# Softmax sums written to PSUM instead of SBUF, and their reciprocals taken in two steps

## The chip, the cores and the metric

The kernel runs on one core of a Trainium2 chip. A core has five engines that work side by side and wait for each other through semaphores: TensorE (PE in the profile; PEld is its loading of weights), VectorE (DVE), ScalarE (ACT), GpSimd (POOL) and SyncE (SP), which issues the transfers between the chip's memory and SBUF. TensorE writes its results to PSUM, eight banks of 2 KB in each of 128 partitions; VectorE and ScalarE read and write both PSUM and SBUF. The metric is the time of one execution on the device, in microseconds (us).

## The reference

The input `x` and the context are 128 batch rows of 128 tokens by 256 features. The attention has 16 heads of 16 features. Its softmax runs over axis 2, the queries (not the keys), so each key has a sum of its own:

```python
x = x + xattn(layernorm(x), ctx, Wq, bq, Wkv, bkv, Wo, bo)
    scores = einsum('bhqd,bhkd->bhqk', q, k) / sqrt(D)
    attn = softmax(scores, axis=2)               # over the queries
    out = einsum('bhqk,bhkd->bhqd', attn, v) @ Wo + bo
x = x + ffn(layernorm(x), w_router, w_block)
    top_idx = top_k(x @ w_router, 96 of 128 tokens)
    out = x with gelu(x[top_idx] @ w_block) put at top_idx
```

## The kernel before

A batch row is one step of a pipeline. Stage offsets are written into the loops by hand: in step s TensorE makes the scores of row s, transposes the inputs of row s + 5, makes the values of row s - 1, keys of row s + 2 or queries of row s + 3 (every other step), the output projection of row s - 2, the product with the block weights of row s - 4, and the attention of row s - 1. Each engine has its own instruction list in the order of the code, and carries it out in that order; nothing is scheduled at run time. A wait holds up everything behind it on its engine.

**Scores and softmax.** `scores(b)` (line 325) makes scores with the keys on the 128 partitions and the queries along the free axis. Its 16 heads lie in four blocks j = 0 to 3 of four heads, each block in one bank of `ps_s`: banks 1 to 3 for blocks 1 to 3 of every row; block 0 changes between bank 0 (even rows) and bank 4 (odd rows), as `bank(b, j)` says. VectorE takes each block's negated maximum over the queries (`maxima`, line 712), in the order 3, 2, 1, 0. ScalarE follows in the same order (`exps`, line 567): four exponentials a block, one for a head, 128 values on each partition, with the maximum as a bias. Each has an `accum_out`: the sum of its 128 results. On the chip that is a pair of instructions, the exponential (ACTIVATE) and the read of the accumulator (ACTIVATION_READ_ACCUMULATOR). The sums of a row lie in the SBUF tile `sums`, four rows deep. The fourth read of a block raises `exp_ready[j]`.

**The reciprocal.** Since the sum belongs to the key, the kernel divides the values and not the probabilities: VectorE takes the reciprocal of all 16 sums of row s - 1 in step s (`inverse_sums`, line 757), GpSimd multiplies the values with it (`values_over_sums`, line 1042), and the attention matmuls (line 402) use them.

**What holds the scores.** `scores(b)` may write its banks when row b - 1 has been read from them. As block 1 is the third to be done, a wait for `exp_ready[1]` covers blocks 3, 2 and 1; block 0 lies in the other bank.

**The router.** Every eighth step a group of eight rows goes through the choice of the 96 tokens. TensorE transposes the group's scores (`candidates`, line 481) into `ps_s`' fifth bank, VectorE finds the 32 smallest in four rounds of max and replace, spread over steps, and TensorE transposes the flags back (`keep_columns`, line 488). Both transposes wait for `exp_ready[0]`, since that bank also holds block 0 of odd rows.

A step of VectorE ends with `final` (line 868, the selected rows), `stats2` (line 735), `product_scaled` (line 815), and the next step begins with `x1_transposed` (line 721), statistics and the router's work, and then `maxima(s, 3)`.

Of the kernel before, what the change touches and what calls it, by code (L numbers as in the profile page):

```python
# [6 lines left out]
def cross_attention_routed_ffn(  # L7
# [40 lines left out]
    with ctx:  # L48
# [3 lines left out]
        def sem(name):  # L52
            return ctx.enter_context(nc.semaphore(name))
# [42 lines left out]
        sums = sb("sums", [P, 4, H])  # L96
# [25 lines left out]
        def bank(b, j):  # L122
            return J if j == 0 and b % 2 == 1 else j

# [49 lines left out]
        recip_ready = sem("recip_ready")  # L174
# [103 lines left out]
        def _(pe):  # L278
# [46 lines left out]
            def scores(b):  # L325

                if not has(b):
                    return
                r2, h = (b // 2) % 2, b % 2
                if b == 0:  # L330
                    pair_ready(b)
                if has(b - 1):
                    pe.wait_ge(exp_ready[1], upto(b - 1))
                for c in range(C):
                    for j in range(J):
                        rows = slice(32 * j, 32 * j + 32)
                        mm = nc.tensor.matmul(ps_s[:, bank(b, j), c, :, :], k_sb[rows, r2, c, h * T:(h + 1) * T],  # L337
                                              q_eo[rows, r2, :, c, h, :], start=True, stop=True)
                        if c == C - 1:
                            mm.then_inc(s_mm[j], 1)  # L340
# [134 lines left out]
            def candidates(b):  # L475

                if b % GROUP == 0 and has(b):
                    pe.wait_ge(z_ready, upto(b + 7))
                    pe.wait_ge(exp_ready[0], upto(b + 11))
                    r = b % R  # L480
                    nc.tensor.transpose(ps_cand, z_sb[:, r:r + GROUP, E], ident[:, :]).then_inc(score_mm, 8)

            def keep_columns(b):

                if b % GROUP == 0 and has(b):
                    pe.wait_ge(keep_row_ready, upto(b + 7))
                    pe.wait_ge(exp_ready[0], upto(b + 15))
# [63 lines left out]
        def _(act):  # L551
# [5 lines left out]
            def exps(b, j, settled=False):  # L557
# [6 lines left out]
                for c in range(C):  # L564
                    for par in range(2):
# [3 lines left out]
                                                    accum_out=sums[:, b % 4, h:h + 1])  # L569
# [108 lines left out]
        def _(dve):  # L678
# [73 lines left out]

            def inverse_sums(b):

                if has(b):
                    dve.wait_ge(exp_ready[0], upto(b))
                    nc.vector.reciprocal(recip[:, b % 4, :], sums[:, b % 4, :]).then_inc(recip_ready, 1)  # L757
# [141 lines left out]
            centre_block_weights()  # L899
            maxima(1, 3)  # L900
# [10 lines left out]
            queries(4)  # L911

            for s in range(2, B):
# [30 lines left out]
                final(s - 16, sure)  # L944
                stats2(s - 2)
# [264 lines left out]
```

## Time and profile before

| | us |
|---|---|
| median of 3 runs | 921.12 (920.46 to 921.23) |
| profiled execution, span from first to last instruction | 919.4 |
| TensorE busy | 889.4 (97%) |
| ScalarE busy | 879.5 (96%) |
| VectorE busy | 873.5 (95%) |
| GpSimd busy | 796.8 (87%) |
| exponentials, 2048, mean 411 ns | 719.1 |
| accumulator reads, 2048, mean 251 ns | 513.5 |
| reciprocals, 128, mean 238 ns | 30.4 |

The median and the range are times of runs without a profile; the span is that of one profiled execution, 1.7 us below the median. Instructions of one engine overlap in the profile: the next one starts before the last one's result is written. The exponentials and the reads add up to more than ScalarE's busy time for that reason. How long an instruction keeps its engine is read from the distance of two starts, and when its result is there from its own duration. In the rows of the section below "start us, us, engine line op out<-in xcount [idle before <-releaser]" are the columns of instructions in order of time; numbers of the form 128x512 are partitions by elements.

### The profile page before, as it was taken

The page shows a single profiled execution, that of the slowest core. Times are in us where ns is not written, and L with a number is a line of the kernel's source. Part 1 is how long each engine was busy: PE and PEld are TensorE (multiplying, and loading weights), DVE is VectorE, ACT ScalarE, POOL GpSimd, SP SyncE. Part 2 cuts the span into 40 slices and gives each one's busy share as a digit, 9 for nine tenths or more (in the row PEclk, how much of TensorE's full clock was granted, in tenths as well). Part 3 has the DMA queues.
Part 4 walks back from the last instruction along what each step waited for, and adds up shares of the span by engine and source line. Part 5 has one row for each costly group of instructions (what it writes and reads, how often), then busy time and mean ns, then how long its engine had stood idle before and what let it go on. Part 6 is the DMA issues. An engine that isn't in the chain of part 4 may idle for free. (4 is left out here: it accounts for less than half of the span.)

```text
span 919.4 us, 31003 instructions
## 1 busy us (share of the span) xinstructions
PE 889.4 (97%) x10306; PEld 753.9 (82%) x10306; DVE 873.5 (95%) x2320; ACT 879.5 (96%) x4503; POOL 796.8 (87%) x1488
## 2 busy tenths in 40 slices
PE   7899999999999999999999999999999999999973
PEld 6788888888888888888888888888888888888861
DVE  6899999999999999999999999999999999999887
ACT  5999999999999999999999999999999999999983
POOL 4568789999989999899999999999899999998865
PEclk9999999999999999999999999999999999999997
DMA  6222123223223223223223223223223222221102
GB/s 198 62 65 71 46 61 95 57 84 93 57 84 95 60 83 92 58 86 91 70 75 91 59 86 91 71 74 89 76 71 89 76 71 87 76 61 53 49 24 92
DMA packets 70976, 70.45 MB, mean 77 GB/s; under 512 B 12064, under 2 KB 62752, under 8 KB 70816
## 3 DMA queue, kind: packets, MB, share of 16 engines
q1 hardware_dynamic: 69456, 67.68, 25.5%
q8 instruction: 82, 1.34, 0.6%
q10 hardware_dynamic: 1360, 0.79, 0.3%
q14 instruction: 78, 0.64, 0.2%
HBM read 35.13 MB, written 16.78 MB: 56 GB/s over the span
## 5 line engine op out<-in xcount | busy, mean ns | idle before, releaser
L567 ACT ACTIVATE e_sb<-ps_s,neg_max 128x128 f32<-128x128 f32 x2048 | 719.1, 411 | 4.4 <-DVE neg_max L712 3.9
L567 ACT ACTIVATION_READ_ACCUMULATOR e_sb<-ps_s,neg_max 128x1 f32 x2048 | 513.5, 251 | 0.0
L712 DVE TENSOR_REDUCE neg_max<-ps_s 128x4 f32<-128x512 f32 x512 | 329.0, 663 | 26.4 <-PE ps_s L337 26.4
L337 PE MATMUL ps_s<-q_eo,k_sb 32*128 32x256 f32 x2048 | 146.6, 400 | 1.1 <-DVE k_sb L790 0.5
L402 PE MATMUL ps_a<-e_sb,v_pad 128*32 128x128 f32 x4096 | 138.4, 276 | 2.2 <-DVE x_sb L729 1.6
L299 PE MATMUL ps_a<-w_o_sb,o_sb 128*128 128x256 f32 x512 | 133.2, 382 | 2.0 <-DVE v_sb L803 1.9
L299 PE MATMUL ps_t<-w_z_sb,xt_sb 128*128 128x258 f32 x512 | 132.6, 381 | 1.3 <-DVE z_sb L815 1.3
L1042 POOL TENSOR_TENSOR v_pad<-v_sb,recip 128x256 f32<-128x256 f32 x128 | 79.6, 622 | 54.0 <-DVE recip L757 52.5
L402 PEld LDWEIGHTS ps_a<-e_sb,v_pad 128*32 128x32 f32 x4096 | 104.1, 109 | 24.0 <-issue 21.6
L337 PEld LDWEIGHTS ps_s<-q_eo,k_sb 32*128 32x128 f32 x2048 | 92.5, 184 | 29.4 <-ACT e_sb L567 17.0
L1031 POOL TENSOR_TENSOR x_sb<-x_sb,bo_sb 128x256 f32<-128x256 f32 x128 | 114.0, 892 | 0.2
L299 PEld LDWEIGHTS ps_t<-w_z_sb,xt_sb 128*128 128x128 f32 x512 | 97.3, 191 | 15.4 <-issue 1.8
L299 PEld LDWEIGHTS ps_a<-w_o_sb,o_sb 128*128 128x128 f32 x512 | 88.0, 189 | 10.1 <-issue 2.4
L1088 POOL TENSOR_TENSOR g_sb<-g_sb,z_sb 128x256 f32<-128x256 f32 x128 | 90.9, 710 | 0.3
L578 ACT CAST t_hi<-ps_t 128x512 fp32r<-128x512 f32 x126 | 74.2, 589 | 14.0 <-PE ps_t L366 10.5
L764 DVE TENSOR_TENSOR t_lo<-ps_t,t_hi 128x512 fp32r<-128x512 f32 x126 | 85.2, 676 | 1.4 <-ACT t_hi L578 1.4
L292 PE MATMUL ps_a<-w_v_hi,t_hi 128*128 128x256 f32 x256 | 84.4, 330 | 1.7 <-ACT o_sb L586 1.6
L1102 POOL TENSOR_TENSOR z_sb<-g_sb,z_sb 128x256 f32<-128x256 f32 x121 | 82.8, 685 | 0.0
L1071 POOL TENSOR_TENSOR g_sb<-z_sb 128x256 f32<-128x256 f32 x123 | 75.6, 614 | 0.3 <-DVE z_sb L815 0.3
L292 PE MATMUL ps_q<-t_hi,w_k_hi 128*128 128x256 f32 x252 | 71.2, 282 | 1.6 <-DVE q_raw L777 1.6
L292 PE MATMUL ps_a<-w_v_lo,t_hi 128*128 128x256 f32 x256 | 72.5, 283 | 0.0
L292 PE MATMUL ps_q<-t_hi,w_q_hi 128*128 128x256 f32 x256 | 72.3, 282 | 0.2 <-DVE t_lo L764 0.2
(102 smaller groups left out, 2197.6 us busy)
## 6 DMA issues: line engine op xcount, KB each, us to landing
x_sb<-in_x SPq DMA_DIRECT2D x64, 256.0 KB, 2.9
c_sb<-in_ctx SPq DMA_DIRECT2D x64, 256.0 KB, 3.1
out<-z_sb SPq DMA_DIRECT2D x64, 256.0 KB, 2.4
q_eo<-q_raw SPq DMA_DIRECT2D x504, 32.0 KB, 2.0
z_sb<-in_L_xattn_Wkv ACTq DMA_DIRECT2D x2, 256.0 KB, 7.2
z_sb<-in_L_xattn_Wq ACTq DMA_DIRECT2D x1, 256.0 KB, 4.5
w_z_sb<-in_L_ffn_w_block SPq DMA_DIRECT2D x1, 256.0 KB, 7.6
w_o_sb<-in_L_xattn_Wo SPq DMA_DIRECT2D x1, 256.0 KB, 7.0
```

Source lines behind the costliest of these rows:

```text
L292: last = nc.tensor.matmul(dst, lhs(a, c), rhs(b, c), start=(c == 0 and n == 0), stop=(c == C - 1 and n == len(terms) - 1))
L299: last = nc.tensor.matmul(dst, lhs(c), rhs(c), start=(c == 0), stop=(c == C - 1))
L337: mm = nc.tensor.matmul(ps_s[:, bank(b, j), c, :, :], k_sb[rows, r2, c, h * T:(h + 1) * T], q_eo[rows, r2, :, c, h, :], start=True, stop=True)
L402: mm = nc.tensor.matmul(ps_attn[32 * j:32 * j + 32, c * T:(c + 1) * T], v_pad[:, b % 2, c * J + j, par:par + 2, :].rearrange("p a d -> p ( ...
L567: last = nc.scalar.activation(e_sb[:, b % 4, j, c, par, :], ps_s[:, bank(b, j), c, par, :], ACT.Exp, bias=neg_max[:, b % 4, h:h + 1], accu ...
L712: nc.vector.tensor_reduce(neg_max[:, b % 4, :].rearrange("p (c j q) -> p j c q", c=C, j=J)[:, j, :, :], ps_s[:, bank(b, j), :, :, :], AX.X ...
L764: nc.vector.tensor_tensor(t_lo[part].rearrange("p k c t -> p (k c) t"), inputs_bank(b)[:, :].rearrange("p (n t) -> p n t", t=T), t_hi[part ...
L1031: nc.gpsimd.tensor_tensor(x_sb[:, b % R, :], x_sb[:, b % R, :], bo_sb[:, :], ALU.add).then_inc(xb_ready, 1)
L1042: nc.gpsimd.tensor_tensor(v_pad[:, b % 2, :, 0:3:2, :], v_sb[:, b % 2, :].rearrange("p (g q d) -> p g q d", q=2, d=D), recip[:, b % 4, :]. ...
L1071: nc.gpsimd.tensor_tensor(g_sb[:, b % 4, :], z_sb[:, b % R, 0:E], z_sb[:, b % R, 0:E], ALU.mult).then_inc(square_ready, 1)
L1088: nc.gpsimd.tensor_tensor(g_sb[:, b % 4, :], g_sb[:, b % 4, :], z_sb[:, b % R, 0:E], ALU.mult).then_inc(cubic_ready, 1)
L1102: nc.gpsimd.tensor_tensor(z_sb[:, b % R, 0:E], g_sb[:, b % 4, :], z_sb[:, b % R, 0:E], ALU.mult).then_inc(gelu_ready, 1)
```

## The change

Each exponential's sum is written into its own block of scores in PSUM, at the first column, which that exponential has just read. The tile `sums` goes. As the next row's scores overwrite banks 1 to 3, the reciprocals of blocks 1 to 3 are taken as 12 values after `final(s - 16)` in step s (`inverse_sums_123`), and the scores of the next row wait for them (`recip_123_ready`) in place of `exp_ready[1]`. Block 0's four are taken in the place of the old reciprocal, in the next step; the two router transposes wait for these (`recip_ready`) in place of `exp_ready[0]`.

```diff
+        def sums_of(b, js):
+            return ps_s[:, bank(b, js[0]):bank(b, js[0]) + len(js), :, :, 0]
...
             def scores(b):
                 if has(b - 1):
-                    pe.wait_ge(exp_ready[1], upto(b - 1))
+                    pe.wait_ge(recip_123_ready, upto(b - 1))
...
             def candidates(b):
-                    pe.wait_ge(exp_ready[0], upto(b + 11))
+                    pe.wait_ge(recip_ready, upto(b + 11))
             def keep_columns(b):
-                    pe.wait_ge(exp_ready[0], upto(b + 15))
+                    pe.wait_ge(recip_ready, upto(b + 15))
...
             def exps(b, j, settled=False):
-                                                    accum_out=sums[:, b % 4, h:h + 1])
+                                                    accum_out=ps_s[:, bank(b, j), c, par, 0:1])
...
+            def inverse_sums_123(b):
+                if has(b):
+                    dve.wait_ge(exp_ready[1], upto(b))
+                    nc.vector.reciprocal(recip[:, b % 4, :].rearrange("p (c j q) -> p j c q", c=C, j=J)[:, 1:J, :, :],
+                                         sums_of(b, (1, 2, 3))).then_inc(recip_123_ready, 1)
             def inverse_sums(b):
                 if has(b):
                     dve.wait_ge(exp_ready[0], upto(b))
-                    nc.vector.reciprocal(recip[:, b % 4, :], sums[:, b % 4, :]).then_inc(recip_ready, 1)
+                    nc.vector.reciprocal(recip[:, b % 4, :].rearrange("p (c j q) -> p j c q", c=C, j=J)[:, 0:1, :, :],
+                                         sums_of(b, (0,))).then_inc(recip_ready, 1)
...
             centre_block_weights()
+            inverse_sums_123(0)
             maxima(1, 3)
...
             queries(4)
+            inverse_sums_123(1)
             for s in range(2, B):
...
                 final(s - 16, sure)
+                inverse_sums_123(s)
                 stats2(s - 2)
```

VectorE's list around a step's end, in a step with router work, before (`z_sb<-z_sb` is the selection of final rows, `neg_max<-ps_s` the maxima, `recip` the reciprocal; the names behind "waits" are semaphores):

```order
L757 RECIPROCAL recip<-sums 128x16 [waits exp_ready0]
L712 TENSOR_REDUCE neg_max<-ps_s 128x2x2 [waits s_mm1]
L777 TENSOR_TENSOR q_raw<-ps_q,bq_sb 128x512 [waits q_mm]
L729 TENSOR_TENSOR x_sb<-ps_a,x_sb 128x256 [waits o_mm]
L712 TENSOR_REDUCE neg_max<-ps_s 128x2x2 [waits s_mm0]
L841 MAX top<-cand 8x8 [waits top_dropped]
L868 SCALAR_TENSOR_TENSOR z_sb<-z_sb,half_keep,x_sb 128x256 [waits u_ready]
L735 BN_STATS st<-x_sb 128x6 [waits x1_ready]
```

The same piece now:

```order
L767 RECIPROCAL recip<-ps_s 128x2x2 [waits exp_ready0]
L715 TENSOR_REDUCE neg_max<-ps_s 128x2x2 [waits s_mm1]
L788 TENSOR_TENSOR q_raw<-ps_q,bq_sb 128x512 [waits q_mm]
L732 TENSOR_TENSOR x_sb<-ps_a,x_sb 128x256 [waits o_mm]
L715 TENSOR_REDUCE neg_max<-ps_s 128x2x2 [waits s_mm0]
L852 MAX top<-cand 8x8 [waits top_dropped]
L879 SCALAR_TENSOR_TENSOR z_sb<-z_sb,half_keep,x_sb 128x256 [waits u_ready]
L760 RECIPROCAL recip<-ps_s 128x3x2x2 [waits exp_ready1]
L738 BN_STATS st<-x_sb 128x6 [waits x1_ready]
```

The reciprocal of 16 values has become one of four in its place, and one of twelve between the selection and the statistics, with a wait for ScalarE's block 1.

VectorE's list at the start, before, from the statistics ahead of row 2's key bias (`k_sb`) over the centring of the block weights (`w_z_sb`) to row 1's first maxima, and then from the query bias (`q_raw`) to row 2's first maxima:

```order
L790 TENSOR_TENSOR k_sb<-ps_q,bk_sb 128x512 [waits k_mm]
L704 TENSOR_TENSOR w_z_sb<-w_z_sb,ps_a 128x258 [waits w_mean_mm]
L704 TENSOR_TENSOR w_z_sb<-w_z_sb,ps_a 128x258
L712 TENSOR_REDUCE neg_max<-ps_s 128x2x2 [waits s_mm3]
...
L777 TENSOR_TENSOR q_raw<-ps_q,bq_sb 128x512 [waits q_mm]
L712 TENSOR_REDUCE neg_max<-ps_s 128x2x2 [waits s_mm3]
```

The same now:

```order
L801 TENSOR_TENSOR k_sb<-ps_q,bk_sb 128x512 [waits k_mm]
L707 TENSOR_TENSOR w_z_sb<-w_z_sb,ps_a 128x258 [waits w_mean_mm]
L707 TENSOR_TENSOR w_z_sb<-w_z_sb,ps_a 128x258
L760 RECIPROCAL recip<-ps_s 128x3x2x2 [waits exp_ready1]
L715 TENSOR_REDUCE neg_max<-ps_s 128x2x2 [waits s_mm3]
...
L788 TENSOR_TENSOR q_raw<-ps_q,bq_sb 128x512 [waits q_mm]
L760 RECIPROCAL recip<-ps_s 128x3x2x2 [waits exp_ready1]
L715 TENSOR_REDUCE neg_max<-ps_s 128x2x2 [waits s_mm3]
```

Twice a reciprocal has been put ahead of a row's first maxima, behind what VectorE does there.

TensorE's order is what it was; the semaphores in two places of it are others. Before (`ps_s<-q_eo` are the scores, `keep_row` the router's flags):

```order
L402 MATMUL ps_a<-e_sb,v_pad 32x128 x15
L337 MATMUL ps_s<-q_eo,k_sb 128x256 [waits exp_ready1]
...
L488 MATMUL ps_s<-ident,keep_row 128x8 [waits exp_ready0,keep_row_ready]
L299 MATMUL ps_a<-w_o_sb,o_sb 128x256 [waits v_ready]
L299 MATMUL ps_a<-w_o_sb,o_sb 128x256
```

And now:

```order
L405 MATMUL ps_a<-e_sb,v_pad 32x128 x15
L340 MATMUL ps_s<-q_eo,k_sb 128x256 [waits recip_123_ready]
...
L491 MATMUL ps_s<-ident,keep_row 128x8 [waits recip_ready,keep_row_ready]
L302 MATMUL ps_a<-w_o_sb,o_sb 128x256 [waits v_ready]
L302 MATMUL ps_a<-w_o_sb,o_sb 128x256
```

Both waits have moved from ScalarE's exponentials to VectorE's reciprocals.

## Rows read from the trace of the kernel before

**Rows 1.** Windows: busy us of each engine (instructions), TensorE clock, DMA, GB/s.

```profile
500.00:600.00 100.00, 100.00 (x1183) 84.75 (x1181) 97.77 (x260) 98.77 (x515) 92.74 (x173) 1.00 0.29 84
```

**Rows 2.** In order of time: TensorE's scores in two following steps.

```profile
502.80 1.15 PE L337 MATMUL ps_s<-q_eo,k_sb 32*128 32x256 f32 x16
...
509.58 1.15 PE L337 MATMUL ps_s<-q_eo,k_sb 32*128 32x256 f32 x16
```

**Rows 3.** Waits of the run: engine, line, waited for, us in total, times, longest.

```profile
DVE neg_max L712 <- PE ps_s L337: 26.4, 76, 0.9
...
PEld ps_s L337 <- ACT e_sb L567: 17.0, 82, 0.7
```

**Rows 4.** In order of time: weight loads of the scores in another step.

```profile
104.87 0.74 PEld L337 LDWEIGHTS ps_s<-q_eo,k_sb 32*128 32x128 f32 x16 [0.20 <-issue]
```

**Rows 5.** In order of time: ScalarE's exponentials and accumulator reads of one step.

```profile
505.05 0.37 ACT L567 ACTIVATE e_sb<-ps_s,neg_max 128x128 f32<-128x128 f32 x1
505.31 0.20 ACT L567 ACTIVATION_READ_ACCUMULATOR e_sb<-ps_s,neg_max 128x1 f32 x1
505.41 0.37 ACT L567 ACTIVATE e_sb<-ps_s,neg_max 128x128 f32<-128x128 f32 x1
...
509.08 0.28 ACT L567 ACTIVATION_READ_ACCUMULATOR e_sb<-ps_s,neg_max 128x1 f32 x1
...
511.84 0.37 ACT L567 ACTIVATE e_sb<-ps_s,neg_max 128x128 f32<-128x128 f32 x1
```

**Rows 6.** In order of time: VectorE, around the reciprocal and the step's end.

```profile
506.32 0.23 DVE L757 RECIPROCAL recip<-sums 128x16 f32<-128x16 f32 x1
506.48 0.62 DVE L712 TENSOR_REDUCE neg_max<-ps_s 128x4 f32<-128x512 f32 x1
...
509.14 0.41 DVE L735 BATCH_NORM_STATS2 st<-x_sb 128x6 f32<-128x256 f32 x1
...
513.17 0.23 DVE L757 RECIPROCAL recip<-sums 128x16 f32<-128x16 f32 x1
...
513.87 0.14 DVE L851 SCALAR_TENSOR_TENSOR drop_rstd<-ps_s,rstd 128x8 f32<-128x8 f32 x1
513.94 0.14 DVE L852 TENSOR_SCALAR half_keep<-ps_s 128x8 f32<-128x8 f32 x1
```

**Rows 7.** The chain that ended last: start us, us, what; between TensorE and ScalarE.

```profile
899.08 0.02 issue
```

**Rows 8.** In order of time: VectorE in two steps with router work.

```profile
324.31 0.41 DVE L735 BATCH_NORM_STATS2 st<-x_sb 128x6 f32<-128x256 f32 x1
...
331.01 0.41 DVE L735 BATCH_NORM_STATS2 st<-x_sb 128x6 f32<-128x256 f32 x1
...
332.81 1.24 DVE L712 TENSOR_REDUCE neg_max<-ps_s 128x4 f32<-128x512 f32 x2
```

**Rows 9.** In order of time: TensorE's scores in these two steps.

```profile
324.40 1.15 PE L337 MATMUL ps_s<-q_eo,k_sb 32*128 32x256 f32 x16
...
331.19 1.15 PE L337 MATMUL ps_s<-q_eo,k_sb 32*128 32x256 f32 x16
```

**Rows 10.** In order of time: TensorE's transpose of the keep flags.

```profile
513.41 0.22 PE L488 MATMUL ps_s<-ident,keep_row 8*128 8x8 f32 x1
```

**Rows 11.** In order of time: VectorE at the start.

```profile
23.08 0.75 DVE L704 TENSOR_TENSOR w_z_sb<-w_z_sb,ps_a 128x258 f32<-128x258 f32 x2
...
30.51 0.67 DVE L777 TENSOR_TENSOR q_raw<-ps_q,bq_sb 128x512 f32<-128x512 f32 x1
```

**Rows 12.** In order of time: TensorE's scores of the second and third row.

```profile
23.39 1.15 PE L337 MATMUL ps_s<-q_eo,k_sb 32*128 32x256 f32 x16
...
30.25 0.93 PE L337 MATMUL ps_s<-q_eo,k_sb 32*128 32x256 f32 x12 [0.46 <-ACT e_sb L567]
```

**Rows 13.** In order of time: TensorE's scores near the end.

```profile
879.53 1.15 PE L337 MATMUL ps_s<-q_eo,k_sb 32*128 32x256 f32 x16
...
885.91 1.15 PE L337 MATMUL ps_s<-q_eo,k_sb 32*128 32x256 f32 x16
```

More of the change, by code:

```diff
@@ L95, in cross_attention_routed_ffn @@
         neg_max = sb("neg_max", [P, 4, H])
-        sums = sb("sums", [P, 4, H])
         recip = sb("recip", [P, 4, H])
@@ L173, in cross_attention_routed_ffn @@
         exp_ready = [sem(f"exp_ready{j}") for j in range(J)]
-        recip_ready = sem("recip_ready")
+        recip_ready, recip_123_ready = sem("recip_ready"), sem("recip_123_ready")
         v_mm = sem("v_mm")
```

## The prediction

> **What bounds the kernel now.** I read the time by stretches first, then the queue of the engine that is never idle, then the list of waits, then the other engines beside that queue.
>
> In the middle of the run TensorE is busy 100 of 100 us, ScalarE 98.77, VectorE 97.77, at a granted clock of 1.00 (the upper of its two levels, 2.4 GHz) [rows 1]. Three engines close to full can all be the bound, so the busy shares decide nothing. What does is who waits. One batch row (a "step" below) takes TensorE from one set of scores at 502.80 us to the next at 509.58 us: 6.78 us [rows 2]. Its matmuls follow each other through that whole step. VectorE, by contrast, waits for TensorE's scores: 26.4 us in 76 places [rows 3]. The list also names ScalarE as what TensorE's weight loads for the scores wait for, 17.0 us in 82 places [rows 3]; I don't believe that. The same load after the same 0.20 us of idle time (17.0 / 82 = 0.21) stands in other steps with no releaser at all [rows 4], so the gap belongs to that change of work on TensorE, and its matmuls run through it. Nor was ScalarE late there: its last accumulator read of the block that frees the scores ends at 509.08 + 0.28 = 509.36 us [rows 5], 0.22 us before the scores start. So TensorE sets the pace, ScalarE has some slack, and VectorE has little: where it waits it has 26.4 / 76 = 0.35 us to spare, and in the steps that also run the router it has none, since there its reduce of the scores comes late and without a wait.
>
> Shortening ScalarE alone therefore gains next to nothing in the middle. The question is what the new reciprocals cost VectorE, and whether TensorE must wait for them.
>
> **The change, part by part.**
>
> *The accumulator read.* An exponential starts 0.26 us before its read and the read 0.10 us before the next exponential: 0.36 us a pair in this first one, 0.34 over the following ones (from 505.05 to 509.08 there are eleven pairs and one exponential: (509.08 - 505.31) / 11 = 0.343) [rows 5]. The read's destination moves from SBUF to PSUM. No ScalarE instruction of this trace writes PSUM, so its saving lies between 0 and the whole 0.09 us; a loss isn't excluded, but nothing points to one. I take 0.04, near the middle. Twelve pairs, to the end of block 1, then take 0.48 us less and sixteen 0.64 us less. As ScalarE isn't the bound, this only pays for the next two points.
>
> *Two reciprocals for one.* The single one occupies VectorE from 506.32 to 506.48: 0.16 us for 16 values, its result 0.23 us after its start [rows 6]. A small VectorE instruction that reads PSUM, 8 values wide, frees the engine after 513.94 - 513.87 = 0.07 us [rows 6]. With 0.07 as the fixed part, 0.09 is left for 16 values; 12 values take 0.07 + 0.07 = 0.14, 4 take 0.07 + 0.02 = 0.09. That is 0.23 for 0.16: +0.07 us a step. Bounds: two at the fixed part alone, 2 x 0.07 = 0.14 (-0.02), and two as long as the old one, 0.32 (+0.16). I take +0.07, the row with PSUM being the nearest.
>
> The Trainium skill speaks against this edit: "VectorE: DVE Perf Modes", section "The TRN2 errata", gives VectorE a fixed 58 cycles from SBUF and 120 from PSUM at 0.96 GHz. By my estimate from it each reciprocal would cost 0.065 us more, +0.20 us a step in all. The 0.07 us row from PSUM doesn't bear that out, but it isn't a reciprocal; the case is a rival below.
>
> *The wait on VectorE for block 1.* The first reciprocal stands behind the selection of final rows and ahead of the statistics, where VectorE arrives at 509.14 us [rows 6]. ScalarE finished that block at 509.36. With eleven pairs 0.04 shorter it ends at 508.92, ahead of VectorE: no wait. Without the shortening VectorE waits 0.22 us, and everything queued behind it (statistics, scaling of the block product, the copy of the transposed row, the next two reduces of the scores) waits too.
>
> *TensorE's wait for the reciprocal instead of block 1.* In the ordinary step the reciprocal starts at 509.14, its result stands 0.21 later, at 509.35, and with 0.05 for the way to TensorE (the chain of waits shows 0.02 between two engines [rows 7]; I allow more, for the weight load) TensorE may go on at 509.40, before its 509.58. Nothing is lost. In router steps VectorE is later. It reaches the place at 324.31 and 331.01 us, while the scores start at 324.40 and 331.19 [rows 8, 9]; a result 0.26 later would come at 324.57 and 331.27, so 0.17 and 0.08 late. Followed through a group of eight steps (router work is repeated every eighth), with VectorE's delay D against today: the last step before 324 has 0.16 - 0.09 = 0.07 less, so TensorE loses 0.10 at the first place. From there each step adds 0.07 to D and VectorE has no idle time to swallow it: 0.07, 0.14, 0.21, 0.28. The next places fit inside TensorE's own delay. At the group's end the transpose of the keep flags (513.41 us) now waits for the second reciprocal, which starts at 513.17 today [rows 6, 10]: 513.17 + 0.28 + 0.15 (its result, 0.23 less 0.07 and rounded) + 0.09 (semaphore and weight load, an allowance) = 513.69, 0.28 late. TensorE's loss is the largest of these, not their sum: 0.28 us a group. Of the sixteen groups fourteen have their keep flags ahead of the last scores: 14 x 0.28 = +3.9 us.
>
> *Start.* The second row's scores started at 23.39 us; they now wait for a reciprocal behind the centring of the block weights, two instructions that began at 23.08 and lasted 0.75 [rows 11, 12]. Freed at about 23.75, plus 0.26: 24.01, 0.62 late. The third row's scores, at 30.25, now stand behind the query bias at 30.51, which takes 0.60: 31.11 + 0.26 = 31.37, 1.12 late [rows 11, 12]. The two overlap, and shorter exponentials give some back: +1.2 us.
>
> *End.* The last steps are 6.38 us apart [rows 13] and have no inputs left to transpose; there ScalarE's chain sets the pace. Twelve pairs give 0.48 back, the detour over VectorE takes 0.26: 0.2 a step, three steps, -0.6 us.
>
> Sum: 3.9 + 1.2 - 0.6 = +4.5 us on the profiled execution (span 919.4 us). The median of the runs is 921.12, 1.7 above that span; I leave the 1.7 as it is. 921.1 + 4.5 = 925.6 us.
>
> **Rivals.**
>
> *The read is no cheaper in PSUM.* Its 0.09 may be the wait for the accumulator, whatever the destination. Then the loop over ScalarE closes: 505.05 to 509.36 is 4.31, the reciprocal's result 0.21 and its two semaphores 0.07, scores to the next exponential 511.84 - 509.58 = 2.26 [rows 2, 5]: 6.85 against 6.78, +0.07 in ordinary steps; in router steps it runs over VectorE's queue, 0.14 for the reciprocal, 1.80 from 331.01 to the reduce at 332.81, 0.62 for that and 0.07 for semaphores [rows 6, 8], to 6.94, +0.16. Four steps of each make 0.9 us a group, 14 groups 12.6; the start in full +1.7, the end 0.26 in three steps +0.8: 15.1, 936 us. For it: no row shows the saving. Against it: the price would fall on every step.
>
> *Dear reciprocals.* With +0.20 a step instead of +0.07, D reaches 0.80 at the keep flags and TensorE loses about 0.85 a group: 12 us, plus the start's 1.2: 934 us.
>
> *Absorbed.* With both reciprocals at the low bound D stays at or below zero; start and end alone remain, +0.6: 921.7 us.
>
> *Faster.* If the 0.20 us gap ahead of the scores were a real wait for ScalarE after all, the 17.0 us would come back, less what VectorE adds (128 x 0.07 = 9): 913 us. For it: the label on 82 gaps. Against it: the equal gaps without a label.
>
> **How the numbers follow.** Forecast 0.41 (its own range 922 to 931, from 0 to 0.5 us a group and a start of 0.6 to 1.5), no cheaper read 0.24 (932 to 943), dear reciprocals 0.10, absorbed 0.17, faster 0.08. A change of 0.2% (1.8 us) is about what can be told from none. Faster: 0.08 and 0.04 of the absorbed case, 0.12. Same: 0.12 of the absorbed and 0.05 of the forecast, 0.17. Slower: the rest, 0.71. The range, 918.5 to 939, leaves out the faster case and the upper half of the dearest one.
>
> **What would show it.** Right: pairs of about 0.30 us; scores still 6.78 us apart in ordinary steps; a group of eight steps 0.2 to 0.4 us longer, with the loss at the scores after the router starts and at the keep flags; reciprocals that free VectorE after 0.14 and 0.09. Wrong in the first step: pairs still 0.34 apart, VectorE waiting for ScalarE ahead of the first reciprocal in every step, and steps of 6.85 or more. Wrong in the second: a reciprocal of 12 values near 0.2. The whole reading is wrong if TensorE's ordinary step gets shorter than 6.77.

## The result and the profile after

The changed kernel takes 925.08 us (median of 4 runs, 924.06 to 925.77), the kernel before 921.17 (4 runs, 920.46 to 921.65); the ratio is 1.004, 95% interval [1.0027, 1.0052]. So it is slower by 3.9 us, against 4.5 forecast. The profiled executions differ by less: a span of 922.3 us against 919.4, 2.9 more. The four runs of the changed kernel are two pairs: at a mean granted clock of 0.994, that of the profiled one, they took 924.06 and 924.38 us, at 0.992 both took 925.77; and where the profiled execution of a kernel below had 0.992 or less (e1, e4, e7, e9, e10), the column "rest" of the table below is 1.4 us or more longer than the changed kernel's 79.73.

The first view is the windows in the middle of the changed kernel [rows 1]; the columns are busy us and instructions of TensorE, of its weight loads, VectorE, ScalarE and GpSimd, then clock, DMA share and GB/s.

```profile
500.00:600.00 100.00, 99.59 (x1151) 85.08 (x1150) 99.18 (x274) 91.95 (x510) 92.64 (x173) 1.00 0.28 78
```

ScalarE has fallen from 98.77 to 91.95, VectorE has risen from 97.77 to 99.18, and TensorE is no longer busy throughout. The list of waits shows who waits for whom now [rows 3]:

```profile
ACT t_hi L581 <- PE ps_t L369: 69.0, 124, 1.6
...
PEld ps_s L340 <- DVE recip L760: 18.6, 75, 1.7
...
PEld ps_s L340 <- issue: 10.3, 52, 0.2
...
DVE neg_max L715 <- PE ps_s L340: 5.1, 9, 1.3
DVE recip L760 <- ACT e_sb L570: 4.7, 13, 0.4
...
PE ps_s L491 <- DVE recip L767: 3.8, 14, 1.2
```

ScalarE waits for TensorE once a step, 69.0 / 124 = 0.56 us. VectorE's waits for scores have gone from 26.4 us to 5.1. New is the last row: in 14 places the transpose of the keep flags stands still until the second reciprocal, 3.8 / 14 = 0.27 us. The wait of the weight loads for the scores (`ps_s L340`) is mostly new in name only: its two rows are 28.9 us in 127 places. The list of before has 17.0 us in 82 places under ScalarE's name [rows 3], and 45 more without one:

```profile
PEld ps_s L337 <- issue: 8.9, 45, 0.2
```

That is 25.9 us, also in 127 places. So the scores' new wait for the first reciprocal is the 3.0 us of difference, and not the 18.6.

The accumulator read, in order of time, ScalarE [rows 5]:

```profile
508.72 0.44 ACT L570 ACTIVATE e_sb<-ps_s,neg_max 128x128 f32<-128x128 f32 x1
508.97 0.25 ACT L570 ACTIVATION_READ_ACCUMULATOR e_sb<-ps_s,neg_max 128x1 f32 x1
509.02 0.46 ACT L570 ACTIVATE e_sb<-ps_s,neg_max 128x128 f32<-128x128 f32 x1
```

The exponential holds ScalarE 0.25 us as before, the read 0.05 instead of 0.09: a pair takes 0.30 us, not 0.343. The Trainium skill ("ScalarE: Activation LUTs", section "Step-by-step: what each stage is for") calls PSUM the faster destination of an ACTIVATE. The trace agrees with that for the time in which the read holds the engine, but not for the length of its own row, 291 ns on the mean against 251 before. No run here tells the cause.

The two reciprocals, VectorE [rows 6]:

```profile
504.93 0.21 DVE L760 RECIPROCAL recip<-ps_s 128x12 f32<-128x12 f32 x1
505.07 0.36 DVE L738 BATCH_NORM_STATS2 st<-x_sb 128x6 f32<-128x256 f32 x1
...
508.91 0.16 DVE L767 RECIPROCAL recip<-ps_s 128x4 f32<-128x4 f32 x1
509.00 0.65 DVE L715 TENSOR_REDUCE neg_max<-ps_s 128x4 f32<-128x512 f32 x1
```

They free VectorE after 0.14 and 0.09 us, the two estimates of the forecast.

Two steps of each group of eight have names below: in the candidate step TensorE transposes the group's scores for the router, and four steps later, in the keep-flag step, it transposes the flags back. The keep-flag step, TensorE and then VectorE [rows 2, 10]:

```profile
505.25 1.15 PE L340 MATMUL ps_s<-q_eo,k_sb 32*128 32x256 f32 x16
512.04 1.15 PE L340 MATMUL ps_s<-q_eo,k_sb 32*128 32x256 f32 x16
516.12 0.19 PE L491 MATMUL ps_s<-ident,keep_row 8*128 8x8 f32 x1 [0.20 <-DVE recip L767]
519.40 1.15 PE L340 MATMUL ps_s<-q_eo,k_sb 32*128 32x256 f32 x16
...
515.81 0.16 DVE L767 RECIPROCAL recip<-ps_s 128x4 f32<-128x4 f32 x1
```

The ordinary step in front of it takes 6.79 us (6.78 before); this one 7.36. Before, the scores behind the keep flags started at

```profile
516.72 1.15 PE L337 MATMUL ps_s<-q_eo,k_sb 32*128 32x256 f32 x16
```

which is 7.14 us after 509.58 [rows 2]. The transpose starts 516.12 - 512.04 = 4.08 us after the scores, before the change 513.41 - 509.58 = 3.83: 0.25 late.

The start [rows 12] and the end [rows 13] of TensorE's scores:

```profile
23.77 1.15 PE L340 MATMUL ps_s<-q_eo,k_sb 32*128 32x256 f32 x16 [0.56 <-DVE recip L760]
31.54 0.71 PE L340 MATMUL ps_s<-q_eo,k_sb 32*128 32x256 f32 x8 [1.39 <-DVE recip L760]
...
882.62 1.15 PE L340 MATMUL ps_s<-q_eo,k_sb 32*128 32x256 f32 x16
888.92 1.15 PE L340 MATMUL ps_s<-q_eo,k_sb 32*128 32x256 f32 x16
```

Both early scores wait for the reciprocal, the second until 1.29 us later than before. At the end two sets are 6.30 apart, not 6.38. That is the last of three steps for which the forecast took 0.2 us each; the other two gave 0.05 and nothing. Most of the gain at the end, 0.39 us, is in the step ahead of these three (6.78 before, 6.39 now).

All kernels are compared below by three numbers of their traces: the start of the 17th set of scores, the mean length of a group of eight steps (start of the 121st set less that of the 17th, divided by 13), and what is left from the 121st set to the end of the span.

| kernel | us, median | before, same chip | ratio, 95% interval | 17th scores | group | rest |
|---|---|---|---|---|---|---|
| before | 921.17 | | | 125.24 | 54.905 | 80.38 |
| changed | 925.08 | 921.17 | 1.0040 [1.0027, 1.0052] | 126.41 | 55.086 | 79.73 |
| e1 split, sums in SBUF | 936.68 | 920.34 | 1.0181 [1.0167, 1.0195] | 128.76 | 55.793 | 82.35 |
| e2 PSUM sums, unused | 916.56 | 920.34 | 0.9959 [0.9946, 0.9971] | 124.34 | 54.700 | 79.59 |
| e5 e2 with the split | 917.62 | 921.14 | 0.9961 [0.9947, 0.9975] | 124.34 | 54.697 | 79.74 |
| e3 early start | 922.50 | 920.34 | 1.0025 [1.0015, 1.0035] | 124.98 | 55.085 | 79.73 |
| e4 early second reciprocal | 919.52 | 920.34 | 0.9993 [0.9984, 1.0002] | 126.60 | 54.735 | 81.17 |
| e6 first reciprocal twice | 929.05 | 921.14 | 1.0084 [1.0070, 1.0098] | 127.05 | 55.412 | 79.99 |
| e7 copy on ScalarE | 925.84 | 921.14 | 1.0046 [1.0034, 1.0059] | 126.00 | 55.089 | 81.16 |
| e8 before, copy on ScalarE | 930.51 | 921.14 | 1.0100 [1.0086, 1.0114] | 126.27 | 55.536 | 80.58 |
| e9 short bias | 924.14 | 920.28 | 1.0045 [1.0030, 1.0059] | 127.00 | 55.086 | 81.29 |
| e11 e3 and e4 | 917.84 | 920.28 | 0.9976 [0.9967, 0.9985] | 124.83 | 54.733 | 79.69 |
| e10 e11 and the copy | 917.85 | 920.28 | 0.9978 [0.9969, 0.9986] | 124.33 | 54.760 | 81.13 |
| e12 e11, first reciprocal first | 953.07 | 920.28 | 1.0357 [1.0343, 1.0370] | 124.58 | 57.368 | 80.86 |

The times in the second column are medians over several runs; the last three columns are of one profiled execution each. The kernels ran on different chips, so times are compared through the ratio to the kernel before on the same chip.

### The profile page after: what moved, and what is told of

Same layout as the page of the kernel before. It is cut to its first block and busy times, and to the rows that moved or that the text cites. A ratio compares the mean times of both kernels' runs of the same rounds, so it can differ in the third digit from the quotient of the medians.

```text
span 922.3 us, 31131 instructions
## 1 busy us (share of the span) xinstructions
PE 888.7 (96%) x10306; PEld 753.2 (82%) x10306; DVE 888.4 (96%) x2448; ACT 821.6 (89%) x4503; POOL 798.4 (87%) x1488
## 3 DMA queue, kind: packets, MB, share of 16 engines
q8 instruction: 82, 1.34, 0.6%
## 5 line engine op out<-in xcount | busy, mean ns | idle before, releaser
L570 ACT ACTIVATE e_sb<-ps_s,neg_max 128x128 f32<-128x128 f32 x2048 | 659.8, 479 | 10.0 <-DVE neg_max L715 9.9
L570 ACT ACTIVATION_READ_ACCUMULATOR e_sb<-ps_s,neg_max 128x1 f32 x2048 | 554.8, 291 | 0.0
L715 DVE TENSOR_REDUCE neg_max<-ps_s 128x4 f32<-128x512 f32 x512 | 332.7, 670 | 8.6 <-PE ps_s L340 5.1
L340 PE MATMUL ps_s<-q_eo,k_sb 32*128 32x256 f32 x2048 | 146.6, 400 | 2.9 <-DVE recip L760 1.9
L1045 POOL TENSOR_TENSOR x_sb<-x_sb,bo_sb 128x256 f32<-128x256 f32 x128 | 121.4, 950 | 0.2
L340 PEld LDWEIGHTS ps_s<-q_eo,k_sb 32*128 32x128 f32 x2048 | 92.5, 184 | 32.4 <-DVE recip L760 18.6
L589 ACT COPY o_sb<-ps_a 128x256 f32<-128x256 f32 x128 | 78.9, 616 | 2.3 <-PE ps_a L405 2.3
L612 ACT ACTIVATE g_sb<-g_sb 128x256 f32<-128x256 f32 x128 | 78.5, 613 | 0.9 <-POOL g_sb L1102 0.9
```

The source lines that it names most:

```text
L570: last = nc.scalar.activation(e_sb[:, b % 4, j, c, par, :], ps_s[:, bank(b, j), c, par, :], ACT.Exp, bias=neg_max[:, b % 4, h:h + 1], accu ...
L589: nc.scalar.copy(o_sb[:, b % 2, :], ps_attn).then_inc(o_ready, 1)
L715: nc.vector.tensor_reduce(neg_max[:, b % 4, :].rearrange("p (c j q) -> p j c q", c=C, j=J)[:, j, :, :], ps_s[:, bank(b, j), :, :, :], AX.X ...
L1045: nc.gpsimd.tensor_tensor(x_sb[:, b % R, :], x_sb[:, b % R, :], bo_sb[:, :], ALU.add).then_inc(xb_ready, 1)
```

## The experiments

**What the two halves are worth.** e1 makes the split and the new waits without PSUM: `accum_out` writes `sums` in SBUF again and both reciprocals read it.

```diff
-                                                    accum_out=ps_s[:, bank(b, j), c, par, 0:1])
+                                                    accum_out=sums[:, b % 4, h:h + 1])
...
```

> The split reciprocals and the new waits of the changed kernel, with the sums accumulated in SBUF as before. Theory (the cheaper accumulator read pays for the detour over VectorE): pairs back at 0.34 us, the last exponential of block 1 about 0.5 us later, VectorE waits for ScalarE ahead of the 12-value reciprocal in most steps, ordinary steps 6.85 us or more, 932 to 938 us. Rival (the read's saving is off the path, the loss is VectorE's extra time and TensorE's wait alone): ordinary steps 6.78, 924 to 926 us.

Measured 936.68 us. The waits of e1, in us, times, longest:

```profile
PEld ps_s L341 <- DVE recip L761: 39.4, 126, 1.9
...
DVE recip L761 <- ACT e_sb L571: 26.1, 60, 0.8
```

VectorE waits for ScalarE ahead of the first reciprocal in 60 steps and the scores for that reciprocal in nearly all; a pair takes 0.343 us again on the mean, ordinary steps are 6.87 us apart, a group takes 0.89 us more than before. This is the rival "no cheaper read" built: it was worked out at 6.85, 0.9 a group and 936 us. The theory stands: without the 0.04 us a pair the detour over VectorE costs 16 us.

e2 is the other half alone: the sums go to PSUM, and the one reciprocal of 16 values reads a constant in SBUF.

```diff
-                                                    accum_out=sums[:, b % 4, h:h + 1])
+                                                    accum_out=ps_s[:, bank(b, j), c, par, 0:1])
...
+            nc.vector.memset(sums[:, :, :], 64.0)
```

> The kernel before with the sums accumulated into PSUM and nothing else: one reciprocal of 16 values of a constant in SBUF, so the weights are not divided by their sums; waits as before. Theory: only what ScalarE's lateness cost comes back, 0.13 us in the one step of eight where the values matmuls start late and 0.2 us a step in the last three, 14 x 0.13 + 0.6 = 2.4: 918 to 919.5 us, ordinary steps still 6.78. Rival (ScalarE was the bound, the gap ahead of the scores a wait for it): ordinary steps below 6.7, 913 us or less. Second rival (the read's time is hidden everywhere): 921 us.

Measured 916.56 us, 3.8 less than before; expected were 2.4. The ordinary steps stay at 6.78, so ScalarE was not the bound there; but a group falls from 54.905 to 54.700. The largest part is one step of eight, the second behind the candidate step. Before, ScalarE came late there with its copy of the attention's result, for which TensorE's matmuls for the values (`w_v_hi`) wait: the copy ended at 332.29 + 0.47 = 332.76, and the first matmul started at 332.81, 1.62 us after the scores at 331.19 [rows 9]; in e2 it is 331.06 - 329.57 = 1.49. ScalarE's copy and the matmul before, then the scores and the matmul in e2:

```profile
332.29 0.47 ACT L586 COPY o_sb<-ps_a 128x256 f32<-128x256 f32 x1
332.81 0.39 PE L292 MATMUL ps_a<-w_v_hi,t_hi 128*128 128x256 f32 x1
...
329.57 1.15 PE L337 MATMUL ps_s<-q_eo,k_sb 32*128 32x256 f32 x16
331.06 0.36 PE L292 MATMUL ps_a<-w_v_hi,t_hi 128*128 128x256 f32 x1
```

The mean of this step is 6.924 before and 6.787 now (0.137). Another 0.07 comes from the keep-flag step, the candidate step and one more. The gap ahead of the scores, which the list of before put down to ScalarE in 82 of 127 places [rows 3, 4], is still there at 0.20 us and has lost its label. In the waits:

```profile
PEld ps_s L337 <- issue: 24.5, 124, 0.2
```

and in order of time:

```profile
110.77 0.74 PEld L337 LDWEIGHTS ps_s<-q_eo,k_sb 32*128 32x128 f32 x16 [0.20 <-issue]
```

**VectorE's time or TensorE's waits.** e5 adds to e2 the two reciprocals at their new places (of the constant; the first one also at the start, for rows 0 and 1), but TensorE waits for the exponentials as before.

```diff
...
                 final(s - 16, sure)
+                inverse_sums_123(s)
                 stats2(s - 2)
```

> The kernel with PSUM sums whose reciprocals read a constant in SBUF (e2, 916.6 us, 54.70 us a group of eight steps), with that reciprocal split into 12 and 4 values at the changed kernel's places, but TensorE waiting for ScalarE's exponentials as before; the weights are not divided by their sums. Theory (the loss of 0.39 us a group against e2 is TensorE's waits for the two reciprocals, not the time that they take): 54.70 to 54.75 us a group, 916.5 to 917.5 us. Rival (VectorE's extra time alone brings the loss): 54.9 us a group or more, 919.5 us or more.

Measured 917.62 us and 54.697 us a group: the split costs nothing. In the keep-flag step (TensorE's scores and transpose, then VectorE) one sees why:

```profile
397.80 1.15 PE L337 MATMUL ps_s<-q_eo,k_sb 32*128 32x256 f32 x16
401.62 0.22 PE L488 MATMUL ps_s<-ident,keep_row 8*128 8x8 f32 x1
404.93 1.15 PE L337 MATMUL ps_s<-q_eo,k_sb 32*128 32x256 f32 x16
...
399.42 1.24 DVE L712 TENSOR_REDUCE neg_max<-ps_s 128x4 f32<-128x512 f32 x2
401.65 0.15 DVE L764 RECIPROCAL recip<-sums 128x4 f32<-128x4 f32 x1
```

VectorE is as late here as in the changed kernel (its reduces start 399.42 - 397.80 = 1.62 us after the scores, there 1.53 on the mean), and the transpose goes ahead at +3.82, before the reciprocal has even begun. The changed kernel's loss against e5, 55.086 - 54.697 = 0.39 us a group, is therefore in TensorE's waits and not in VectorE's work; the one other difference is that e5's reciprocals read SBUF. e5 also prices the source: started to next instruction, the reciprocals take 0.138 and 0.085 us from SBUF (medians), 0.143 and 0.090 from PSUM in the changed kernel.

**Each wait by itself.** e3 moves the two reciprocals of the start up.

```diff
+            inverse_sums_123(0)
             centre_block_weights()
-            inverse_sums_123(0)
...
-            for b in range(8, 10):
-                stats1(b)
-                aggregate1(b)
+            stats1(8)
+            aggregate1(8)
+            inverse_sums_123(1)
+            stats1(9)
+            aggregate1(9)
             queries(4)
-            inverse_sums_123(1)
```

> The changed kernel with the 12-value reciprocals of rows 0 and 1 moved ahead of the centring of the block weights and of the query bias. Theory: the start's 1.1 us comes back and nothing else: 923.7 to 924.3 us, the fourth set of scores about 1.2 us earlier than in the changed kernel. Rival (the start is made up for later anyway, the steps cost more than read): 925 us.

Measured 922.50 us, a ratio of 1.0025 for the changed kernel's 1.0040: 1.4 us. (It lies under the expected range because this chip ran the kernel before in 920.34 us, not in 921.17.) The third scores start at 30.07 and wait 0.41, not 1.39; the group is unchanged. The 1.4 us are saved once and stay saved: the span is 920.8, 1.5 less than the changed kernel's.

```profile
30.07 1.15 PE L340 MATMUL ps_s<-q_eo,k_sb 32*128 32x256 f32 x16 [0.41 <-DVE recip L760]
```

e4 moves the second reciprocal up. GpSimd's scaling of the values, which waits for it, must then also wait for the values in every step.

```diff
                 maxima(s, 2)
+                inverse_sums(s - 1)
                 router(s - 16, 9)
                 values_and_bias(s - 1, sure)
                 inputs_low(s + 5)
-                inverse_sums(s - 1)
...
                     pool.wait_ge(recip_ready, upto(b))
-                    if not settled:
-                        pool.wait_ge(v_ready, upto(b))
+                    pool.wait_ge(v_ready, upto(b))
```

> The changed kernel with the 4-value reciprocal moved up behind the first two reduces of the scores, ahead of the value bias and the low parts of the inputs (0.93 us of VectorE earlier); GpSimd's scaling then waits for the value bias too. Theory (the keep flags' transpose waits for that reciprocal, 0.2 us in each eighth step): that step returns from 7.37 to 7.15 us, 14 x 0.2 = 2.8 less: 921.5 to 923 us. Rival (VectorE is busy 99 of 100 us and has itself become the bound, whatever waits where): the 0.2 turns up in another step of the eight, 924.5 to 925.5 us.

Measured 919.52 us, 0.9993 of before [0.9984, 1.0002]; more than the 2.8 us expected, since the group falls by 0.35, 4.6 us in 13 groups. TensorE's scores and transpose of the keep flags, and VectorE's reciprocal:

```profile
400.26 1.15 PE L340 MATMUL ps_s<-q_eo,k_sb 32*128 32x256 f32 x16
404.07 0.22 PE L491 MATMUL ps_s<-ident,keep_row 8*128 8x8 f32 x1
407.38 1.15 PE L340 MATMUL ps_s<-q_eo,k_sb 32*128 32x256 f32 x16
...
402.84 0.16 DVE L767 RECIPROCAL recip<-ps_s 128x4 f32<-128x4 f32 x1
```

The reciprocal now starts 1.2 us before the transpose, which starts at +3.81 unhindered: 0.24 back in this step. The other 0.12 comes from the step with the candidates (7.010 to 6.886): 0.04 ahead of their transpose, which has the same reciprocal to wait for, and 0.085 ahead of the scores behind it, which wait for the first reciprocal, and that one e4 did not move. It came earlier because GpSimd did. VectorE's selection of final rows and the first reciprocal behind it, then GpSimd's addition of the bias, in the candidate step of the changed kernel and of e4:

```profile
325.49 0.74 DVE L879 SCALAR_TENSOR_TENSOR z_sb<-z_sb,half_keep,x_sb 128x256 f32<-128x256 f32 x1
326.14 0.22 DVE L760 RECIPROCAL recip<-ps_s 128x12 f32<-128x12 f32 x1
325.21 0.73 POOL L1045 TENSOR_TENSOR x_sb<-x_sb,bo_sb 128x256 f32<-128x256 f32 x1
...
324.31 0.46 DVE L879 SCALAR_TENSOR_TENSOR z_sb<-z_sb,half_keep,x_sb 128x256 f32<-128x256 f32 x1
324.69 0.21 DVE L760 RECIPROCAL recip<-ps_s 128x12 f32<-128x12 f32 x1
323.51 0.73 POOL L1045 TENSOR_TENSOR x_sb<-x_sb,bo_sb 128x256 f32<-128x256 f32 x1
```

In the changed kernel the addition is still running when the selection starts, and the selection holds VectorE 0.65 us; in e4 the addition is over by then, and it holds 0.38. So the 0.35 us are not all due to the shorter wait: some 0.085 come from a collision that GpSimd's earlier start took away. VectorE was busy 99.71 of 100 us in the middle of e4, more than in the changed kernel, and TensorE 100.00: VectorE isn't the bound.

**How much room VectorE has.** e6 takes the first reciprocal twice.

```diff
                     dve.wait_ge(exp_ready[1], upto(b))
+                    nc.vector.reciprocal(spare[:, b % 4, :].rearrange("p (c j q) -> p j c q", c=C, j=J)[:, 1:J, :, :],
+                                         sums_of(b, (1, 2, 3)))
```

> The changed kernel with the 12-value reciprocal taken twice (the first into a spare place). Theory (VectorE is idle only 0.4 us in a group of eight steps; 8 x 0.14 = 1.1 more makes it the bound): 0.7 to 1.1 us more a group, 933 to 940 us. Rival (the loss is only in the two router places, elsewhere there is room): 0.3 us more a group at most, 929 us or less.

Measured 929.05 us, 0.33 more a group for 8 x 0.14 = 1.1 us of work, close to the rival's 0.3. My theory fell here: a busy share of 99% is no sign that an engine is full. From the step behind the keep flags to the candidate step VectorE's first reduce starts 1.29 us after the scores in the kernel before, in the changed one and in e6 (there 1.34 in the first of the four): VectorE catches up in these steps, though hardly any idle time is on record. The loss stands in the steps in which it is late: 0.08 us each in the candidate and the keep-flag step, 0.05 in each of the three between.

e7 takes 0.33 us a step off VectorE: ScalarE makes the copy `xt_sb`, between its tanh and its cast.

```diff
                 gelu_tanh(s - 7)
+                x1_copied(s - 4)
                 inputs_high(s + 5, sure)
...
                 sure = 20 <= s < B - 1
-                x1_transposed(s - 4, sure)
```

> The changed kernel with one 0.33 us VectorE instruction of every step, the copy of the transposed row out of PSUM, moved to ScalarE, ahead of its cast, where ScalarE now waits about 0.5 us for TensorE. Theory (the change made ScalarE idle and VectorE late; moving work over takes the loss away): the keep-flag step back from 7.37 to 7.15 us or less, 54.65 to 54.8 us a group, 917.5 to 919.5 us with the start's loss still in it. Rival (ScalarE's copy comes late or pushes the cast and the exponentials, or the waits stay where they are): 54.95 us a group or more, 922 us or more.

Measured 925.84 us, no gain. VectorE now waits for scores again, yet a new loss stands in the step ahead of the keep flags. VectorE and GpSimd there:

```profile
400.56 0.87 DVE L888 SCALAR_TENSOR_TENSOR z_sb<-z_sb,half_keep,x_sb 128x256 f32<-128x256 f32 x1
401.35 0.22 DVE L769 RECIPROCAL recip<-ps_s 128x12 f32<-128x12 f32 x1
...
400.41 0.73 POOL L1053 TENSOR_TENSOR x_sb<-x_sb,bo_sb 128x256 f32<-128x256 f32 x1
```

The selection of final rows, 0.38 us from start to next elsewhere, takes 401.35 - 400.56 = 0.79 when GpSimd has begun its addition of the bias 0.15 us earlier. VectorE's earliness was eaten there, the first reciprocal behind it came late, and the scores waited for it.

e8 puts the same copy on ScalarE in the kernel before.

> The kernel before with the same copy moved to ScalarE, sums in SBUF. Theory (ScalarE has 1.2 idle us in 100 there, so 0.25 us more a step makes it the bound): 0.1 to 0.2 us more in every step, 932 to 942 us. Rival (the relief of VectorE is worth more): 920 us or less.

Measured 930.51 us, ScalarE busy 100.00 of 100 us (500 to 600), 0.63 more a group: 0.13 to 0.16 in four of the eight steps and little in the others, so the theory's direction at somewhat less than its size. What ScalarE has free in the changed kernel it has not before.

e9 looks at that collision in the changed kernel: GpSimd adds the bias to 16 of 256 columns only.

```diff
-                    nc.gpsimd.tensor_tensor(x_sb[:, b % R, :], x_sb[:, b % R, :], bo_sb[:, :],
+                    nc.gpsimd.tensor_tensor(x_sb[:, b % R, 0:16], x_sb[:, b % R, 0:16], bo_sb[:, 0:16],
```

> The changed kernel in which GpSimd adds the output bias to 16 of 256 columns only (the other columns go without it). In the changed kernel VectorE's selection of final rows takes 0.38 us where GpSimd is at another work and 0.50 to 0.66 where it overlaps this addition: 3.86 us a group of eight steps against 3.45 before. Theory (the change moved VectorE into this collision, and in the step with the candidates that made the 12-value reciprocal late): the selections back at 0.38 to 0.40, the scores behind the candidate step no longer late (0.085 us), the wait at the keep flags smaller but there: 54.85 to 55.0 us a group, 921.5 to 923.5 us. Rival (the collision hides behind other waits): 55.05 to 55.1 us a group, 924 to 925 us.

Measured 924.14 us, the rival's time: inconclusive for the loss, clear for the mechanism. The selection in the candidate step falls from 0.66 to 0.38 and the scores behind it are on time: the step takes 6.925 us, not 7.010. But groups now alternate between 54.85 and 55.35 us, and in the long ones another pair collides (VectorE, GpSimd, TensorE):

```profile
294.81 0.68 DVE L857 TENSOR_SCALAR keep_row<-cand 8x128 f32<-8x128 f32 x1
295.41 0.41 DVE L814 TENSOR_TENSOR v_sb<-ps_a,bv_sb 128x256 f32<-128x256 f32 x1
...
294.79 0.61 POOL L1085 TENSOR_TENSOR g_sb<-z_sb 128x256 f32<-128x256 f32 x1
...
296.65 0.20 PE L491 MATMUL ps_s<-ident,keep_row 8*128 8x8 f32 x1 [0.54 <-DVE recip L767]
```

The keep flags, 0.13 us of work, hold VectorE for 0.60, until GpSimd's instruction ends at 295.40, and TensorE pays 0.54. This agrees with the Trainium skill ("SBUF — State Buffer", section "SBUF: two separate sides"): VectorE and GpSimd share a pair of ports, and when a VectorE instruction uses both ports, or has two inputs in SBUF against a GpSimd instruction that reads SBUF, whichever engine starts first keeps the pair for its whole instruction.

**Putting it together.** e11 is e3 and e4 in one; e10 adds e7's copy; e12 swaps the first reciprocal and the selection of final rows in e11.

> The two mendings together: the start of e3 (1.4 us) and the early 4-value reciprocal of e4 (54.73 us a group). Theory (their gains add): 917.5 to 918.8 us, ratio to before 0.997 to 0.998. Rival (one takes the other's gain): 919.3 us or more.

> The two mendings and the copy of the transposed row on ScalarE. Theory (with the waits on the 4-value reciprocal gone, VectorE's 0.33 us a step let the router steps end on time): 54.65 to 54.72 us a group, 916.5 to 918 us. Rival (as in e7, VectorE now reaches its selection of final rows while GpSimd adds the bias, and loses what it gained): 54.8 us a group or more, 919 us or more.

```diff
+                inverse_sums_123(s)
                 final(s - 16, sure)
-                inverse_sums_123(s)
```

> The two mendings, with the 12-value reciprocal ahead of the selection of final rows instead of behind it. Theory (scores no longer wait for a selection held up by GpSimd: 0.04 us in one step of eight): 0.5 us less than the two mendings alone. Rival (VectorE gets there 0.4 us earlier, waits for ScalarE's block 1 in ordinary steps and is later everywhere): 54.8 us a group or more, 1 us more than the two mendings alone.

e11 takes 917.84 us, 0.9976 of before [0.9967, 0.9985], 2.4 us faster than the kernel before on the same chip: the gains add. Its middle:

```profile
500.00:600.00 100.00, 100.00 (x1191) 85.06 (x1189) 99.72 (x280) 92.13 (x510) 91.67 (x173) 1.00 0.29 82
```

TensorE is full again. e10 is the same within its interval, 917.85 us, as its theory had it in time (its group, 54.760, lies between theory and rival): once TensorE is full, relieving VectorE was worth nothing. e12 loses 35 us, far more than its rival said. Its waits:

```profile
PEld ps_t L369 <- DVE z_sb L826: 55.2, 92, 0.7
...
DVE recip L760 <- ACT e_sb L570: 20.2, 58, 0.6
```

VectorE stands still for ScalarE in 58 steps; the selection behind it then falls into GpSimd's work in seven steps of eight (0.61 to 0.82 us), and the scaled product, later still, holds up the next input transposes 92 times.

## Why the prediction came out, step by step

**The read.** Estimated 0.04 us a pair, measured 0.043. Right in size. "This only pays for the next two points" was wrong, and with it that shortening ScalarE gains next to nothing in the middle: e2 shows that the read alone gives 0.205 us a group, 2.7 us over 13 groups, 0.137 of it in one step of eight in which ScalarE was late for TensorE's values matmuls. I had looked for ScalarE's slack in one ordinary step only.

**The reciprocals.** 0.14 and 0.09 as worked out. The rival of dear reciprocals is out, by the 0.005 us between PSUM and SBUF. Its price was too high as well: for 0.13 us a step more than the forecast's it added 12 - 3.9 = 8 us, and e6, with 0.14 more, lost 13 x 0.33 = 4.2.

**The wait on VectorE for block 1.** Right both ways: with the cheaper read VectorE waits for ScalarE there 13 times in the run; without it (e1) 60 times, at 936.7 us for the 936 computed.

**TensorE's waits.** This is the term that was mis-sized: +0.28 us a group was the forecast, 55.086 - 54.905 = +0.18 was measured. Right was where: the candidate step is 0.09 longer than before (7.010 for 6.917; forecast 0.10), and the other loss is at the keep flags (7.37 for 7.14), with 0.14 between them given back by the cheaper read. Mis-sized was VectorE's delay D against the kernel before. It was to be 0.07, 0.14, 0.21 and 0.28 us in the four steps from the one behind the candidates to the keep flags. Counted from the scores of the candidate step, VectorE's reduces came later than before by -0.01, 0.05, 0.10 and 0.15 (means of ten groups): D begins at nothing and grows by 0.05 a step, not 0.07. At the keep flags that makes 0.15 for D, 0.16 for the reciprocal's result (forecast 0.15) and 515.81 + 0.16 to 516.12, 0.15, for the way to TensorE (forecast 0.09): the transpose comes 0.21 later than before, not 0.28.

Against e5, which has the cheaper read and none of the waits, the changed kernel's loss is larger, 0.39: 0.12 in the candidate step, 0.24 in the keep-flag step, little elsewhere. The forecast had left out that the cheaper read brings TensorE to the keep flags 0.16 us earlier than before (e5, from the scores of the candidate step); an engine that comes earlier to a late result waits longer for it. The 0.12 and the 0.24 are parts of one lateness, so "the largest of these, not their sum" isn't refuted. In e5 the second reciprocal of the keep-flag step is done 4.00 us after the scores and the transpose starts at 3.81 (means); with 0.15 for the way, TensorE would have lost 4.15 - 3.81 = 0.34 by my estimate if it had waited there alone, nearly the 0.36 that it lost in both places. No run has the one wait without the other and all else alike.

Two causes were missing from the forecast. The candidates' transpose waits for the second reciprocal too (0.04 us). And VectorE's selection of final rows collides with GpSimd's addition: 3.86 us a group for the selections instead of 3.45. A cost of that is shown in the candidate step alone, the 0.085 us that e4 and e9 get back; that selection met GpSimd before the change too, but then no scores waited for what stands behind it.

The two errors went opposite ways: 0.39 - 0.205 = 0.18 us a group, and 13 of them 2.35 us, where 0.28 and 3.9 us in 14 had been forecast.

**Start and end.** Forecast +1.2, measured +1.17 up to the 17th scores. The parts are less exact: the second row's scores were 0.38 us late (forecast 0.62), the third's 1.29 (1.12). e3, which moves both reciprocals up, has its 17th scores 1.43 us earlier, so it is those two waits, less what the cheaper read gives back. At the end -0.6 was forecast and -0.65 measured from the 121st scores on, but that is luck: of the three last steps, 0.2 us each by the forecast, one gave 0.05, one nothing and one 0.09, and 0.39 came from the step ahead of them.

Sum on the profiled executions: 1.17 + 2.35 - 0.65 = 2.9, for 4.5 forecast. Between the medians it is 3.9; that this comes nearer to the forecast than the sum of the parts does is luck too.

**The faster rival** is out: the gap labelled with ScalarE is there in e2, where ScalarE is busy 92.3 us of 100, at the same 0.20 us.

Open is why exactly the group stays at 55.09 us in e7 and e9, with different steps late in each; the traces show the collisions, no run shows a rule for where they settle.

## What to carry to other kernels

When a result that another engine waits for is moved behind more work, price the wait, not the work: the two reciprocals cost nothing, waiting for them 0.39 us a group, and moving the second up its engine's queue gave 0.35 of that back, some of it because GpSimd's work moved along. When the same change lets another engine come earlier, it may only wait longer. Look for an engine's slack in every kind of step, not in the commonest one. Before giving VectorE's or GpSimd's work a new place in time, look at what the other does there.

## What the runs showed of the hardware

- ScalarE's accumulator read holds the engine 0.05 us when it writes PSUM (changed kernel, e2) and 0.09 when it writes SBUF (before, e1).
- A VectorE instruction that meets one of GpSimd's can hold its engine much longer: 0.79 for 0.38 us (e7), 0.60 for 0.13 (e9), the latter on 8 partitions.
- A reciprocal of 4 or 12 values takes the same from PSUM as from SBUF, within 0.005 us (e5 and the changed kernel).
- A releaser in the list of waits can be a coincidence: 17.0 us under ScalarE's name in the kernel before went to no name in e2, where ScalarE got faster.
